# Routed experts of a two-layer transformer: the first two products turned round, with the weights as the stationary operand

## The reference

```python
def _swiglu_stacked(x, w1, b1, w2, b2, w3, b3):
    p1 = jnp.einsum('btd,ndh->nbth', x, w1) + b1[:, None, None, :]
    p2 = jnp.einsum('btd,ndh->nbth', x, w2) + b2[:, None, None, :]
    glu = jax.nn.silu(p1) * p2
    return jnp.einsum('nbth,nhd->nbtd', glu, w3) + b3[:, None, None, :]
scores = jax.nn.softmax(x @ gate_w + gate_b, axis=-1)
weights, indices = jax.lax.top_k(scores, K)
routed_all = _swiglu_stacked(x, rw1, rb1, rw2, rb2, rw3, rb3)
...
routed = jnp.sum(weights[..., None] * gathered, axis=2)
```

## Time and profile before

| what | value |
|---|---|
| median of 3 runs | 816.52 us |
| lowest and highest | 815.5 and 820.49 us |
| the profiled execution's own time | 817.38 us |
| its span in the trace | 815.7 us |
| granted TensorE clock, mean | 0.993 |

### The profile page before, as it was taken

How to read it: one execution, slowest core, us unless ns; L and a number is a source line. 1 busy time by engine, 2 the same in 40 slices (tenths; PEclk the granted TensorE clock), 3 DMA queues, 4 the chain that set the end, 5 groups by cost and what they waited for, 6 DMA issues and landing times.

```text
span 815.7 us, 14156 instructions
## 1 busy us (share of the span) xinstructions
PE 760.1 (93%) x5120; PEld 508.1 (62%) x5120; DVE 474.5 (58%) x1102; ACT 264.3 (32%) x524; POOL 277.7 (34%) x296
## 2 busy tenths in 40 slices
PE   6998999999999989989999999999989889999997
PEld 4675656755675555465666566555666666676775
DVE  2548564245734566814444473645658786888754
ACT  1323311241124121102222222222216665554562
POOL 4863615060320240611441433626693222101010
PEclk8999999999999999999999999999999999999999
DMA  9899434342250194844677654686767683662201
GB/s 257 225 307 324 123 104 131 115 133 76 87 176 15 28 375 172 278 126 125 185 201 206 194 177 140 183 251 172 214 178 203 171 224 114 182 182 71 73 2 46
DMA packets 70677, 133.53 MB, mean 164 GB/s; under 512 B 10401, under 2 KB 51362, under 8 KB 68690
## 3 DMA queue, kind: packets, MB, share of 16 engines
q1 hardware_dynamic: 54864, 81.14, 32.2%
q10 hardware_dynamic: 7906, 31.23, 13.9%
q0 software_dynamic: 7840, 20.26, 9.1%
HBM read 104.02 MB, written 28.41 MB: 162 GB/s over the span
## 4 chain that ended last, share of the span: by engine, by line
PE 74%; DVE 14%; ACT 4%; DMA 3%; issue 2%; POOL 1%; ACTq 0%; SPq 0%; DVEq 0%; POOLq 0%
PE ps L1323 14%; PE ps L1015 11%; PE ps L1339 7%; PE ps L1026 6%; PE ps L1036 4%; PE ps L2016 4%; DVE mxh L1662 4%; PE ps L2045 4%; PE ps L2036 3%; PE ps L2009 2%; PE ps L958 2%; PE ps L1330 2%; PE ps L1991 2%; PE ps L992 2%; PE ps L1046 2%
## 5 line engine op out<-in xcount | busy, mean ns | idle before, releaser
L1662 DVE TENSOR_REDUCE mxh<-ps 112x2 f32<-112x750 f32 x128 | 115.3, 934 | 22.9 <-PE ps L2016 21.5
L1323 PE MATMUL ps<-rw,rowsT 128*128 x280 | 126.1, 593 | 0.6 <-ACT rowsT L1282 0.6
L1875 ACT ACTIVATE d_pT<-ps 125x448 f32<-125x448 f32 x192 | 92.1, 548 | 66.9 <-PE ps L2036 63.5
L1015 PE MATMUL ps<-x1T,sw 128*128 128x448 f32 x256 | 102.8, 547 | 6.3 <-DVE gluT L465 4.9
L1323 PEld LDWEIGHTS ps<-rw,rowsT 128*128 128x128 f32 x280 | 50.5, 190 | 51.0 <-issue 51.0
L1015 PEld LDWEIGHTS ps<-x1T,sw 128*128 128x128 f32 x256 | 46.8, 190 | 51.7 <-issue 38.2
L2016 PE MATMUL ps<-kst,qst 96*112 96x375 bf16 x256 | 64.4, 339 | 7.8 <-DVE mxh L1662 2.8
L1339 PE MATMUL ps<-rw,gT 128*128 x280 | 66.4, 380 | 0.8 <-ACT gT L1286 0.8
L1339 PEld LDWEIGHTS ps<-rw,gT 128*128 128x128 f32 x280 | 52.9, 190 | 21.3 <-issue 15.9
L1026 PE MATMUL ps<-sw,gluT 128*112 128x256 f32 x256 | 57.8, 381 | 4.3 <-DVE gluT L465 4.3
L325 POOL DMA_INDIRECT xg<-xh_moe,places x32 | 32.8, 1024 | 83.4 <-DVE places L552 49.1
(11 more groups left out here) (239 smaller groups left out, 1257.2 us busy)
## 6 DMA issues: line engine op xcount, KB each, us to landing
rb<-in_rb SPq DMA_DIRECT2D x35, 512.0 KB, 4.3
kst<-kscr ACTq DMA_DIRECT2D x45, 378.0 KB, 5.2
rw<-in_rw SPq DMA_DIRECT2D x24, 512.0 KB, 9.9
kscr<-ka SPq DMA_DIRECT2D x16, 567.0 KB, 3.7
cT<-in_ctx_t SPq DMA_DIRECT2D x21, 378.0 KB, 5.0
ctxT<-in_ctx_t SPq DMA_DIRECT2D x16, 378.0 KB
ctxn<-in_ctx SPq DMA_DIRECT2D x16, 336.0 KB
qst<-qscr ACTq DMA_DIRECT2D x12, 448.0 KB, 6.8
```

The lines of the kernel that those rows point to most:

```text
L1015: last = mm(bank[up_in(i, m)[k]][:, 0:GS], w[:, e, c, h * P:(h + 1) * P], x1T[:, c, :], start=c == 0, stop=c == C - 1)
L1323: last = mm(bank[1 + 2 * q + k], rowsT[:, q, c * P:(c + 1) * P], w[:, e, c, :], start=c == 0, stop=c == C - 1)
L1662: V.tensor_reduce(mxh[:, 2 * g:2 * g + 2], ps[0:S, p:p + 2, 0:K], axis=AX_X, op=ALU.max).then_inc(s["s_max"], 1)
L1875: A(pT[:, q % 2, k, :], bank[4 + k][0:KC, 0:QUAD * S], ACT.Exp).then_inc(s["p_ready"], 1)
```

## The change

`up` gives the products the other way round. For each of the two weights and each of the HM = 4 blocks of 128 hidden features, the weights' 128x128 block is the stationary operand and the tile's 128 rows of `rowsT` move: 16 products of 128 columns for a tile in place of 4 of 512. The result has the hidden features on the partitions, which is what `down` needs as its stationary operand; so `hidden_T`, `gT_out`, the buffer `gT` and both of their semaphores go, and `down` reads `h2` itself.

The stationary operand is no longer read from `rw1` and `rw2` under a register. ACT reads the expert's number into a register and copies its weights into a fixed buffer `w12` with one copy of 128x1024 floats for each of the two weights (`weights_out`). There is one buffer for each weight: the copy for tile n waits until `up(n - 1)` is done with it. Tile 0's copies wait for the weights' loads.

The bias is now one number for each partition and block: the host lays it out as 128x8 floats for each expert, the load is of 8 floats to each partition, and DVE reads each number for 128 columns in turn. DVE's second addition also waits until `down(n - 2)` has read `h2`.

```diff
-            sp.dma_start(rb12[:, q, :], dram["rb12"][bass.ds(e, 1), :].to_broadcast([P, 2 * H])).then_inc(s[f"bias_in{q}"], 16)
+            sp.dma_start(rb12[:, q, :], dram["rb12"][bass.ds(e, 1), :].rearrange("o (p x) -> (o p) x", p=P)).then_inc(s[f"bias_in{q}"], 16)
...
+        def bias(q, k):
+            return rb12[:, q, k * HM:(k + 1) * HM].unsqueeze(2).to_broadcast([P, HM, P])
...
-            V.tensor_tensor(h1[:, q, :], bank[1 + 2 * q], rb12[:, q, 0:H], ALU.add).then_inc(s["h1_ready"], 1)
+            V.tensor_tensor(by_block(h1[:, q, :]), by_block(bank[1 + 2 * q]), bias(q, 0), ALU.add).then_inc(s["h1_ready"], 1)
             v.wait_ge(s["p2_ps"], n + 1)
-            V.tensor_tensor(h2[:, q, :], bank[2 + 2 * q], rb12[:, q, H:2 * H], ALU.add).then_inc(s["h2_ready"], 1)
+            if n >= 2:
+                v.wait_ge(s["y_ps"], n - 1)
+            V.tensor_tensor(by_block(h2[:, q, :]), by_block(bank[2 + 2 * q]), bias(q, 1), ALU.add).then_inc(s["h2_ready"], 1)
...
-        def gT_out(n):
-            a.wait_ge(s["gT_ps"], n + 1)
-            A(gT[:, n % 2, :], bank[5], ACT.Copy).then_inc(s["gT_ready"], 1)
...
+        def weights_out(n, e, k):
+
+            if n:
+                a.wait_ge(s[("p1_ps", "p2_ps")[k]], n)
+            A(w12[:, k, :, :], (rw1, rw2)[k][:, e, :, :], ACT.Copy).then_inc(s[("w1_ready", "w2_ready")[k]], 1)
+
+        a.wait_ge(tiles_ready, 1)
+        e = expert_of(0)
+        a.wait_ge(weights_in, 3 * 16 * E)
+        for k in range(2):
+            weights_out(0, e, k)
         rowsT_out(0)
         rowsT_out(1)
+        e = expert_of(1)
+        weights_out(1, e, 0)
         silu(0)
+        weights_out(1, e, 1)
         for n in range(LAST):
             if n + 2 < NTILE:
                 rowsT_out(n + 2)
-            gT_out(n)
+                e = expert_of(n + 2)
+                weights_out(n + 2, e, 0)
             silu(n + 1)
+            if n + 2 < NTILE:
+                weights_out(n + 2, e, 1)
             beside(a, n + 1)
-        gT_out(LAST)
...
-            for k, (w, sign) in enumerate(((rw1, "p1_ps"), (rw2, "p2_ps"))):
-                for c in range(C):
-                    last = mm(bank[1 + 2 * q + k], rowsT[:, q, c * P:(c + 1) * P], w[:, e, c, :], start=c == 0, stop=c == C - 1)
+            for k, (ready, sign) in enumerate((("w1_ready", "p1_ps"), ("w2_ready", "p2_ps"))):
+                t.wait_ge(s[ready], n + 1)
+                for m in range(HM):
+                    block = slice(m * P, (m + 1) * P)
+                    for c in range(C):
+                        last = mm(bank[1 + 2 * q + k][:, block], w12[:, k, c, block], rowsT[:, q, c * P:(c + 1) * P], start=c == 0, stop=c == C - 1)
                 last.then_inc(s[sign], 1)
...
-            for m in range(HM):
-                last = nc.tensor.transpose(bank[5][:, m * P:(m + 1) * P], h2[:, q, m * P:(m + 1) * P], ident[:])
-            last.then_inc(s["gT_ps"], 1)
...
-                last = mm(bank[6][:, 0:D], gT[:, q, m * P:(m + 1) * P], rw3[:, e, m, :], start=m == 0, stop=m == HM - 1)
+                last = mm(bank[6][:, 0:D], h2[:, q, m * P:(m + 1) * P], rw3[:, e, m, :], start=m == 0, stop=m == HM - 1)
...
-            hidden_T(n - 1)
-            up(n, ahead)
+            up(n)
             beside(t, n, 0)
             down(n - 1, e)
...
-    out["rb12"] = np.concatenate([a[f0 + "rb1"], a[f0 + "rb2"]], 1)
+    out["rb12"] = np.stack([a[f0 + n].reshape(E, HM, P) for n in ("rb1", "rb2")], 1).transpose(0, 3, 1, 2).reshape(E, P * 2 * HM)
```

More of the change, by code:

```diff
@@ L1196, in _, with routed_experts @@
         second["tensor"](t)
-def routed_experts(nc, tensors, dram, expert_row, row_base, weights, ps, bank, ident, always, tiles_ready, scattered, new_semaphore, pool_semaphore):
+def routed_experts(nc, tensors, dram, expert_row, row_base, weights, weights_in, ps, bank, ident, always, tiles_ready, scattered, new_semaphore, pool_semaphore):
     def sem(name):
@@ L1205, in routed_experts @@
     rw1, rw2, rw3 = weights
-    h1, h2, rows, rowsT, rb12, rb3, y, gT = tensors
+    h1, h2, rows, rowsT, rb12, rb3, y, w12 = tensors
     s = {n: sem("c_" + n) for n in (
         "rows_in0", "rows_in1", "rT_ps", "rT_ready", "p1_ps", "p2_ps", "h1_ready", "silu_ready", "h2_ready",
-        "glu_ready", "gT_ps", "gT_ready", "y_ps", "y_ready", "bias_in0", "bias_in1")}
+        "glu_ready", "y_ps", "y_ready", "bias_in0", "bias_in1", "w1_ready", "w2_ready")}
     s.update({n: pool_semaphore("c_" + n) for n in ("y_out0", "y_out1", "rb3_in0", "rb3_in1")})
@@ L1249, in vector, with by_block @@
         V = nc.vector
+        def by_block(at):
+            return at.rearrange("p (m t) -> p m t", m=HM)
+        def bias(q, k):
+            return rb12[:, q, k * HM:(k + 1) * HM].unsqueeze(2).to_broadcast([P, HM, P])
         def front(n):
@@ L1290, in silu, with expert_of @@
             A(h1[:, n % 2, :], h1[:, n % 2, :], ACT.Silu).then_inc(s["silu_ready"], 1)
+        def expert_of(n):
+            return a.value_load(expert_row[0:1, n:n + 1], min_val=0, max_val=E - 1)
+        def weights_out(n, e, k):
[7 more added lines that the diff above has]
+            weights_out(0, e, k)
         rowsT_out(0)
         rowsT_out(1)
+        e = expert_of(1)
+        weights_out(1, e, 0)
         silu(0)
+        weights_out(1, e, 1)
         for n in range(LAST):
@@ L1316, in expert_of, with up, down @@
             return t.value_load(expert_row[0:1, n:n + 1], min_val=0, max_val=E - 1)
-        def up(n, e):
+        def up(n):
             q = n % 2
             t.wait_ge(s["rT_ready"], n + 1)
-            for k, (w, sign) in enumerate(((rw1, "p1_ps"), (rw2, "p2_ps"))):
-                for c in range(C):
-                    last = mm(bank[1 + 2 * q + k], rowsT[:, q, c * P:(c + 1) * P], w[:, e, c, :], start=c == 0, stop=c == C - 1)
+            for k, (ready, sign) in enumerate((("w1_ready", "p1_ps"), ("w2_ready", "p2_ps"))):
[4 more added lines that the diff above has]
+                        last = mm(bank[1 + 2 * q + k][:, block], w12[:, k, c, block], rowsT[:, q, c * P:(c + 1) * P], start=c == 0, stop=c == C - 1)
                 last.then_inc(s[sign], 1)
-        def hidden_T(n):
+        def down(n, e):
             q = n % 2
             t.wait_ge(s["glu_ready"], n + 1)
-            for m in range(HM):
-                last = nc.tensor.transpose(bank[5][:, m * P:(m + 1) * P], h2[:, q, m * P:(m + 1) * P], ident[:])
-            last.then_inc(s["gT_ps"], 1)
-        def down(n, e):
-            q = n % 2
-            t.wait_ge(s["gT_ready"], n + 1)
             if n:
@@ L1345, in tensor @@
         e = expert_of(0)
-        up(0, e)
+        up(0)
         for n in range(1, NTILE):
@@ L1356, in tensor @@
             e = ahead
-        hidden_T(LAST)
         down(LAST, e)
@@ L2290, in then @@
         def then(first):
+            (w12,) = named(ctx, (("w12", [P, 2, C, H], F32),))
             of_experts = named(ctx, (
                 ("h1", [P, 2, H], F32), ("h2", [P, 2, H], F32),
-                ("rows", [P, 2, D], F32), ("rowsT", [P, 2, C * P], F32), ("rb12", [P, 2, 2 * H], F32), ("rb3", [P, 2, D], F32),
-                ("y", [P, 2, D], F32), ("gT", [P, 2, H], F32)))
+                ("rows", [P, 2, D], F32), ("rowsT", [P, 2, C * P], F32), ("rb12", [P, 2, 2 * HM], F32), ("rb3", [P, 2, D], F32),
+                ("y", [P, 2, D], F32)))
             ahead = named(ctx, (
@@ L2300, in then @@
                 ("qst_0", [P, NH, GS], BF16), ("d_wv1", [P, C, D], F32), ("cT_0", [P, C, KP], F32)))
-            experts, routed = routed_experts(nc, of_experts, dram, expert_row, row_base, weights, ps, bank, ident, always,
+            experts, routed = routed_experts(nc, of_experts + [w12], dram, expert_row, row_base, weights, first["rw_in"], ps, bank, ident, always,
                                              tiles_ready, scattered, sem, sem)
```

## The result

The changed kernel takes 806.15 us (median of 4 runs, 804.99 to 806.86), the kernel before 816.41 beside it (4 runs, 815.5 to 820.49). The ratio is 0.9841, with a 95% interval of 0.9805 to 0.9878. The forecast was 805.0 us. The profiled execution took 806.61 us, its span is 804.9.

The account below looks back on a forecast made before the run. PE, with work for 93% of the span, was taken to bound the kernel. -15.4 + 7.4 - 4.7 + 1.0 = -11.7 us on the profiled 817.38 gave 805.7, or 805.0 us allowing for the median; range 797 to 817.

Parts of the forecast that it names:

- The transposes: `hidden_T` on PE's path in the expert stage: 0.44 us in each of 35 tiles goes, 15.4 us saved.
- `up`: PE's first two products, turned round: 32 pairs at 0.112 us plus 0.07, 3.65 us a tile, +7.4 us in all.
- The first rival: In `up`, part of each load is always added: 820.5 to 829.6 us; chance 0.12 in full, 0.05 by a part.
- The rule named in the prediction: Trainium skill's back-to-back issue gap: load and movement both set spacing, 25 ns more a pair, `up` 4.29 us, a loss.
- The rival of loads that don't overlap: In `up`, each load waits for the products before it: 0.221 us a pair, some 930 us; chance 0.02.
- The copies: ACT's two weight copies a tile, 1.06 us each, hidden with 2.6 us to spare: they cost nothing.
- the third rival: ACT late with a copy where DVE runs behind from second-layer work: 3 to 5 us back, about 809; chance 0.05.
- DVE's repeated bias number: DVE's additions on 128x512 might slow, no row showing that form; the copies' slack covers twice their time.
- Waits that go and come: PE's waits in the expert stage: 4.7 us of idle time goes, 1.0 us comes once at tile 28.
- the wait at tile 28: PE waits for an ACT copy issued behind three transfers: about 0.9 us, counted as +1.0 once, between 0 and 1.4.
- the end of the stage gives back: PE reaches the stage's end 1.5 us sooner and may wait for a second-layer transfer: 806.5 us; chance 0.02.
- The traffic of the biases: 35 x 512 KB of bias transfers leave the rows' queue; the 0.4 us wait for `rows` may go, counted as nothing.

Follow-up runs that it names:

- the kernel with the later splits: Changed kernel with POOL's query splits moved to tiles 26 and 33, the store one tile later, query transfers at tile 30: 820.84 us, ratio 0.9965.

## Why the prediction was right

Forecast 805.0 us, measured 806.15; the gain was 10.3 us by the medians, forecast 11.5. By the interval of the ratio the gain is 10.0 to 15.9 us, so the measurement can't tell the forecast from the sizes below. The mechanism was the predicted one, and two of its sizes were off.

- **The transposes**, -15.4: right. The chain has lost its 0.44 us piece, and putting it back costs 0.44 in each tile.
- **`up`**, +7.4: mis-sized. It is +4.6 (35 x 0.13). The pace of L992's loads, 0.112, was the right row; the 0.07 us for a hand-over, taken over from the same row, doesn't come here: 32 x 0.112 is 3.58, and 3.57 is measured. The value lies inside the stated ends, 3.49 and 3.76.
- **The first rival**, a part of each load always added: fell. It needed 0.122 us a pair. Halving the columns took away at most 0.002 us a pair and nothing from the tile, so there is no such part. The rule named in the prediction, 25 ns for each pair in a stream, doesn't hold for these float32 pairs: 3.57 us, not 4.29. The rival of loads that don't overlap, 7.1 us, fell with it.
- **The copies**, nothing: right in the steady tiles. The length was predicted (1.06 us, measured 1056 ns). The slack, 2.6 us, covered twice the work without lengthening a steady tile. Once, in the last tiles, a copy was late by 0.8 us, by the mechanism of the third rival: DVE behind because of second-layer work.
- **DVE's repeated bias number**, left open: nothing. The additions take 688 and 690 ns, before 692.
- **Waits that go and come**, -4.7 and +1.0: together -3.7 predicted. The stage's -12.9 less -15.4 and +4.6 leaves -2.1. The stops went, though the runs price them at 3.0 us with the transposes in place; the wait at tile 28 came (0.5, predicted 0.9). What the step left out is that PE, arriving earlier at the end of the stage, meets DVE's stretched work and a bias transfer beside the key loads: three waits, 2.4 us. The rival "the end of the stage gives back" had the place and not the transfer: it was the last bias, not the second layer's own loads.
- **The traffic of the biases**, nothing: right to within 1.4 us, by the ratio of 0.9999 and its interval.
- **Outside the stage**, nothing predicted: 2.1 us longer in this pair of executions, where the changed kernel's clock was lower. The 1.3 us at the start are shown above to be that.

2.8 us less for `up`, 1.6 more for waits and 2.1 outside the stage make the profiled gain 10.8 where 11.7 was worked out. Part of the closeness is luck: what `up` gives more is offset by the waits and by the clock of one pair of executions.

## What to carry to other kernels

Where PE sets the time, cost a change of form by the pace of pairs in the chain of waits: the longer of load and movement counts, and in float32 with 128 stationary columns nothing is gained by moving fewer than 128. So turning a product round to make its output what the next product wants costs little down to 128 columns, here 0.13 us a tile, and saves the transposes and their wait. Look at the ends of a stage by themselves: waits there come from other engines' work and from how transfers fall. Before moving a burst of transfers to save a small wait, look at what is issued right behind it in the new place: here a wait of 0.5 us was traded for one of 4 to 5.5. And change one thing at a time, since four kernels here carry that move together with others.

## What the runs showed of the hardware that was not expected

- DVE slows beside POOL's subtractions of two tensors, by operand, and in the kernel before as well (the gates' product takes 2.15 us at 567.19 there). Operations on SBUF alone stretch: the gates' product from 0.69 to 2.30 us (at 512.84, POOL's subtraction at 512.70 for 1.89), four mixes from 1.91 to 5.37. Additions that read PSUM stay at 0.69 (at 526.27 in the kernel before, wholly beside a subtraction). Once it is POOL that is stretched: at 556.38 in the changed kernel both start together, DVE's product takes its 0.69 and POOL's subtraction 2.44 in place of 1.89.
- An idle spell of PE can cost more than its length. In the kernel with the later splits PE has 1.01 us of work between 552.0 and 558.5, and then the granted clock falls. Its windows (stretch, length, PE, PEld, DVE, ACT, POOL, clock, DMA share, GB/s):

```profile
552.00:558.50 6.50, 1.01 (x5) 0.56 (x3) 2.98 (x7) 0.46 (x1) 4.38 (x6) 0.96 0.96 239
558.50:564.00 5.50, 5.45 (x36) 5.42 (x37) 0.74 (x2) 1.96 (x3) 0.00 (x0) 0.73 0.14 46
564.00:570.00 6.00, 6.00 (x46) 5.69 (x45) 4.64 (x9) 3.47 (x5) 1.10 (x2) 1.00 0.17 36
```

  At a mean of 0.73, part 1.2 and part 2.4 GHz, the transposes and `up` take from 558.55 to 563.75, 5.20 us where 3.79 is the rule: 1.4 us on top of the wait of 5.5. It isn't a matter of long spells alone: in two kernels (small bias transfers; three bias buffers) the mean clock is 0.79 in 364 to 372, behind the same short waits after which the kernel before and the changed kernel hold 1.00, and the first `up` takes 1.6 to 1.7 us more. So a difference of this size between two profiles can be the clock's and not the edit's.
- A transfer's landing depends on its neighbours more than on its size: 128 KB of bias take 3.4 us in the median and 5.3 to 8.2 beside the key loads. The rows' 128 KB went from 3.8 to 2.1 when the 512 KB beside them shrank, and take 7.4 to 10.3 behind three query transfers of 448 KB.
